# Hypergraph scatter in four rounded-type products, one attention tile later on TensorE

## The chip, the cores and the metric

The kernel runs on one core of a Trainium2 chip. The metric is the device time of one execution in microseconds; the kernel before takes 1202.09 us, the median of three runs (1201.91 to 1204.01).

## What is computed

The input is `x` of 16 batches x 512 nodes x 128 features and a 512x512 adjacency. Four graph layers follow each other, each with a layer norm, a ReLU and a residual. The edit is in the third, a hypergraph layer over 256 edges with given end nodes `src` and `dst` and 4 heads:

```python
# third layer (cut)
Xq = (H @ W_lin.T).reshape(bt, n, h, dh)
Xv = (H @ W_val.T).reshape(bt, n, h, dh)
e = jnp.einsum('behd,hd->beh', leaky_relu(Xq[:, src] + Xq[:, dst], 0.2), a)
e = e + jnp.log(A0[src, dst] + EPS)[None, :, None]
attn = softmax of e over the edges that share a src      # segment_max, exp, segment_sum
Y = segment_sum(attn[..., None] * Xv[:, dst], src, num_segments=n)   # the scatter
return Y @ W_out.T
```

The first layer is a graph ODE of 8 Euler steps, the second a masked graph attention, the fourth a Chebyshev propagation, a 4-head masked attention over all nodes and a feed-forward part. All work is in float32; where a product is made in the rounded type (float32r), the operand that is not exact in it is split into a rounded part and a rest.

## The kernel before

The program has two parts. The front (about 430 us) prepares tables and does the first layer for all batches, and already the first steps of batch 0. The rest treats the batches in a software pipeline of five stages: `gat`, `edge`, `cheb`, `att` and `ffn`, each one batch behind the one before. Each engine (TensorE is PE, VectorE DVE, ScalarE ACT, GpSimd POOL, and SP for the transfers) has a list of steps, written out by hand. `FILL_ORDER` (line 1685) is run once at the start, `ORDER` (line 1652) is the body of a loop with ten passes, and `DRAIN_ORDER` (line 1779) ends the program. An engine runs its list strictly in order, and a step waits on semaphores for what it needs. So the position of a step in a list decides what it holds up.

The steps around the edit, with their lines:

- `edge_u` (line 308, DVE) writes `U`, 128x256: the weighted values of the 256 edges, in two tiles of 128 edges.
- `edge_scatter` (line 370, PE) multiplies each tile of `U` by `src_rows`, a 0/1 table of 128 edges x 512 nodes, and adds both products in bank `b0`: two float32 products of 128x512. `src_rows` is filled by GpSimd in `edge_tables` (line 740). Earlier, the front keeps other data in the same memory (line 609).
- `edge_yT` (line 257, ACT) copies the result into `hg`, `edge_out` (line 377, PE) multiplies it by `W_out`, and `edge_x3` (line 315, DVE) adds the residual. `edge_x3` is the last DVE step of a pass. The next pass begins on DVE with `cheb_stats`, `cheb_aggr`, `gat_x2a`, `att_rv`.
- `att_turn` 0 to 15 (line 2442, PE) transpose the 16 attention tiles, all into one bank, `c2`. `att_copy` (line 2153, ACT) copies each out, so `att_turn` i waits for `att_copy` i-1. `att_score` (line 2434, PE), `att_mask` (line 2243, DVE) and `att_exp` (line 2145, ACT) make the tiles; each score feeds its mask, the mask its exponential.
- `att_rows` (line 2507, PE), early in the next pass, waits for `att_rv` (line 2318, DVE). `ffn_wo` (line 2529, PE) waits for `att_scale` (line 2322, DVE).
- On GpSimd a pass ends with `n3_rstd`, `ffn_x3b`, `n3_g` and `ffn_final` of the feed-forward stage.
- The edge gather (line 331, PE) already works in the rounded type: rounded part and rest of the nodes against a 0/1 table.

The PE order of a pass near its end is: `gat_pv0 att_turn11 att_score14 edge_scatter att_turn12 att_score15 edge_out att_turn13 gat_pv1 att_turn14 cheb_v`. On ACT it is `att_exp13 att_copy11 att_exp14 edge_yT att_copy12 att_exp15 att_copy13`.

Of the kernel before, what the change touches and what calls it, by code (L numbers as in the profile page):

```python
# [40 lines left out]
def need(eng, sem, value):  # L41
# [8 lines left out]
    edge_x edge_lcol edge_xz edge_le edge_exp edge_scattered edge_yT gat_done edge_stat edge_z edge_lb edge_max  # L50
    edge_lc edge_den edge_rden edge_attn edge_v edge_u x3_stored cheb_h edge_done ffn_y3 gat_turned gat_zloaded
    gat_loaded gat_aggr gat_vareps gat_rs gat_small gat_exp gat_s2 gat_hT gat_wh gat_pv gat_whs gat_max
    gat_eturn gat_eT gat_stat gat_normed gat_T gat_rinv
""".split()


# [5 lines left out]
def build(nc, t_in, out):  # L62
    ctx = ExitStack()
    with ctx:
        def sb(name, shape, dt=F32, c=None):
            return (c or ctx).enter_context(nc.sbuf_tensor(name, shape, dt))

        sems, kept = {}, {}

        def sem(name):  # L70

            if name not in sems:
                sems[name] = nc.alloc_semaphore(f"{name}_start")
# [24 lines left out]
        ones = sb("ones", [P, P])
        lap_hi = sb("lap_hi", [P, NT, N], R32)
        lap_lo = sb("lap_lo", [P, NT, N], R32)  # L100
        mask_gat = sb("mask_gat", [P, NT, N], BF16)
        mask_att = sb("mask_att", [P, NT, N], BF16)
        with ExitStack() as front:
            zsplit = sb("z_split", [P, 2, 2, N], R32, front)
        edge_pick = sb("edge_pick", [P, NT, 2 * E], R32)
        src_rows = sb("src_rows", [P, ET, N])
        seg_bias = sb("seg_bias", [P, ET, E])
        same_src = sb("same_src", [P, ET, E])
        logA = sb("logA", [P, ET])
        W = {n: sb("w_" + n, [P, D]) for n in ["Wc", "Wq", "Wk", "Wv", "Wo", "WlinT", "WvalT", "WoutT"]}  # L110
        W1 = sb("w_W1", [P, HID])
        W2 = sb("w_W2", [P, 2, D])
        rowv = sb("rowv", [P, len(ROWS), D])
        row = {n: rowv[:, i, :] for i, n in enumerate(ROWS)}
        b1c = sb("b1c", [P, 2])
        neg_half = sb("neg_half", [P, NT])
        W1ga = sb("w_W1ga", [P, D + 2])
        W["W1g"] = W1ga[:, 0:D]
        head_a4 = sb("head_a4", [P, H])

        def row4(name, c=NT):
            return row[name].unsqueeze(1).broadcast_to([P, c, D])

        k = Shared(t_in=t_in, out=out, bank=bank, sem=sem, kept_sem=kept_sem, nodes1=nodes1, row=row, row4=row4, W=W, W1=W1, W2=W2,
                   x1_dram=x1_dram, x3_dram=x3_dram, res_dram=res_dram, v_dram=v_dram, rowv=rowv, b1c=b1c,
                   ident=ident, ones=ones, neg_half=neg_half, lap_hi=lap_hi, lap_lo=lap_lo, mask_gat=mask_gat,
                   mask_att=mask_att, zsplit=zsplit, edge_pick=edge_pick, src_rows=src_rows, seg_bias=seg_bias,
                   same_src=same_src, logA=logA, W1ga=W1ga, head_a4=head_a4)

        k["gat"] = gat_memory(nc, ctx)
        k["edge"] = pair_memory(nc, k.gat)
        k["pair_words"] = 3 * NT * N + 4 * NT * D + 3 * E + ET * H * E // 2 + 6 * ET * H + ET * D + (6 + 2 + 4) * NT
        k["gat_steps"] = gat_stage(nc, k, kept_sem)
# [3 lines left out]
        nc.clear_and_free_semaphores(list(sems.values()))  # L140
# [44 lines left out]


def edge_stage(nc, k, sem):  # L190

    g = k.edge
    h2, x3, h2_hi, h2_lo, hg, xz, small, U = g.h2, g.x3, g.h2_hi, g.h2_lo, g.hg, g.xz, g.small, g.U
    zT, YT, x2, W = xz, hg, k.gat.x2, k.W
    b0, b1 = k.bank[4], k.bank[5]

    def cols(t):
        return slice(t * P, (t + 1) * P)
# [4 lines left out]
    def ready(eng, name, n, count=1, per=1):  # L203
        need(eng, sem(name), n * per + count)
# [10 lines left out]
    def on_gpsimd(pool):  # L215
# [13 lines left out]
            nc.gpsimd.tensor_tensor(h2_lo[:], h2[:], h2_hi[:].bitcast(F32), ALU.subtract  # L229
                                    ).then_inc(sem("edge_hlo"), 1)  # L230

        return {"edge_rstd": edge_rstd, "edge_lo": edge_lo}

    def on_scalar(act):
        def edge_apply(n):
# [88 lines left out]
    def on_tensor(pe):  # L324
# [43 lines left out]
            mm.then_inc(sem("edge_den"), 1)  # L368

        def edge_scatter(n):  # L370
            ready(pe, "edge_u", n)
            for e in range(ET):
                mm = nc.tensor.matmul(b0[:], U[:, cols(e)], k.src_rows[:, e, :], start=(e == 0),
                                      stop=(e == ET - 1))
            mm.then_inc(sem("edge_scattered"), 1)

        def edge_out(n):
# [189 lines left out]
def build_front(nc, k):  # L567
# [3 lines left out]
    with ExitStack() as c:  # L571
# [34 lines left out]
        S = [k.lap_hi, k.lap_lo]  # L606
        sqr = k.mask_att[:].rearrange("p t m -> p (t m)")

        gb = [k.src_rows[:].rearrange("p e n -> p (e n)")[:, i * D:(i + 1) * D] for i in range(STEPS)]
        gb.append(k.seg_bias[:, 0, 0:D])  # L610
        node_col = sb("node_col", [P, NT])
        edge_ci = sb("edge_ci", [P, 2, ET], I32)
# [108 lines left out]
        def _(pool):  # L721
# [934 lines left out]
        ffn_up0 att_score6 ffn_up1 att_turn4 att_score7 ffn_down0 ffn_down1 cheb_x1turn att_turn5 att_score8  # L1656
        edge_gather0 att_turn6 edge_gather1 att_score9 cheb_q edge_x att_turn7 att_score10 gat_eturn0 edge_lcol
        edge_lb0 edge_lb1 gat_eturn1 att_turn8 att_score11 cheb_k gat_eturn2 gat_eturn3 att_turn9 att_score12 edge_v
        edge_den att_turn10 att_score13 gat_pv0 att_turn11 att_score14 edge_scatter att_turn12 att_score15 edge_out
        att_turn13 gat_pv1 att_turn14 cheb_v  # L1660
    """.split(),
    "DVE": """
        cheb_stats cheb_aggr gat_x2a+ att_rv+ gat_x2b+ gat_stats att_mask0 gat_aggr edge_stats att_mask1 edge_aggr
# [8 lines left out]
        att_copy1 gat_wh_out1 edge_hi att_exp4 att_copy2 ffn_x2T att_exp5 att_copy3 ffn_gelu0 ffn_gelu1 att_exp6  # L1672
        att_copy4 att_exp7 att_copy5 cheb_x1T att_exp8 att_copy6 edge_hg gat_exp0 cheb_qsplit edge_xz att_exp9
        att_copy7 gat_exp1 gat_exp2 gat_exp3 gat_eT0 att_exp10 gat_eT1 att_copy8 att_exp11 edge_exp att_copy9 gat_eT2
        gat_eT3 cheb_ksplit att_exp12 att_copy10 att_exp13 att_copy11 att_exp14 edge_yT att_copy12 att_exp15
        att_copy13 att_copy14 att_copy15 cheb_vout att_spread
    """.split(),
    "POOL": """
        cheb_rstd gat_rstd edge_rstd ffn_res n2_rstd edge_lo ffn_b2 n1_rstd n3_rstd ffn_x3b n3_g ffn_final
    """.split(),  # L1680
    "SP": """
        load_z load_x3+ stack0+ stack2+ store_out+ load_xr stack1+ stack3+ edge_store+ load_x store_v+ cheb_res load_v
# [83 lines left out]
        cheb_rstd:0 gat_rstd:2 edge_rstd:1 n1_rstd:0 edge_lo:1 cheb_rstd:1 gat_rstd:3 edge_rstd:2 edge_lo:2 n1_rstd:1
        cheb_rstd:2 ffn_res:0 gat_rstd:4 edge_rstd:3 n2_rstd:0 ffn_b2:0 edge_lo:3 n1_rstd:2 n3_rstd:0 ffn_x3b:0 n3_g:0
        ffn_final:0 cheb_rstd:3 ffn_res:1 gat_rstd:5 edge_rstd:4 n2_rstd:1 ffn_b2:1 edge_lo:4 n1_rstd:3 n3_rstd:1
        ffn_x3b:1 n3_g:1 ffn_final:1
    """.split(),  # L1770
    "SP": """
        load_z:2 edge_store:0 cheb_res:0 load_x:2 load_z:3 stack0:0 stack2:0 edge_store:1 stack1:0 load_x:3 stack3:0
# [819 lines left out]
```

## Time and profile before

| | |
|---|---|
| median of 3 runs | 1202.09 us |
| profiled execution, first to last instruction | 1201.4 us |
| PE busy | 1124.4 us (94%) |
| DVE busy | 814.3 us (68%) |
| ACT busy | 759.7 us (63%) |
| POOL busy | 342.6 us (29%) |

The profile counts an instruction as busy from its start to its end. Products on PE overlap: the next one starts before the one before it has ended, so the distance of two starts tells what a product costs PE, and the duration when its result can be used. A float32 product of 128x512 shows as two records, one in the rounded type as one. The idle time that the profile gives before an instruction is put down to what ended it.

### The profile page before, as it was taken

To read this page: it belongs to the slowest core of one execution; us is meant where nothing else is said; L and a number is where in the kernel's file an instruction comes from. 1 tells how busy PE (TensorE), PEld (TensorE's weight loads), DVE (VectorE), ACT (ScalarE), POOL (GpSimd) and SP (SyncE) were. 2 spreads that over 40 slices of the span, in tenths; PEclk is the share of its full clock that TensorE was granted. 3 is DMA by queue.
4 is the path that set the end of the run, shared out by engine and by line. 5 is a ranking of instruction groups with operands and counts; after the bars stand their busy time and mean duration, and the time that the engine had idled before them with its cause. 6 is when DMAs were issued, how large, how long until landed. Compare 5 with 4: busy or idle time off the path is not lost. (4 is left out here: it accounts for less than half of the span.)

```text
span 1201.4 us, 23468 instructions
## 1 busy us (share of the span) xinstructions
PE 1124.4 (94%) x7537; PEld 898.6 (75%) x7537; DVE 814.3 (68%) x2964; ACT 759.7 (63%) x1627; POOL 342.6 (29%) x465
## 2 busy tenths in 40 slices
PE   8999999999999987999999999999999999999685
PEld 5678888889889865777777777777777777766454
DVE  7662222223335567798998988988988988977665
ACT  4324234334113234987988988988988988988762
POOL 3312005003032121133253243243243243243123
PEclk9999999999989998999999999999999999999987
DMA  4020120120110013243343343343343343233420
GB/s 130 24 56 1 45 62 1 45 62 1 56 33 9 28 36 92 71 111 96 90 116 90 88 118 89 88 115 92 88 114 94 88 114 94 81 106 86 122 67 27
DMA packets 132321, 87.85 MB, mean 73 GB/s; under 512 B 13600, under 2 KB 115360, under 8 KB 132256
## 3 DMA queue, kind: packets, MB, share of 16 engines
q1 hardware_dynamic: 132192, 87.02, 26.7%
q8 instruction: 36, 0.59, 0.2%
q14 instruction: 29, 0.24, 0.1%
q0 software_dynamic: 64, 0.00, 0.0%
HBM read 32.45 MB, written 20.97 MB: 44 GB/s over the span
## 5 line engine op out<-in xcount | busy, mean ns | idle before, releaser
L2247 DVE CUSTOM_DVE_ANT_0 att_Ts<-bank,mask_att 128x512 f32<-128x512 f32 x256 | 174.5, 683 | 63.6 <-PE bank L2402 61.2
L2149 ACT ACTIVATE att_Es<-att_Ts,att_small 128x512 f32<-128x512 f32 x256 | 185.4, 724 | 35.0 <-DVE att_small L2247 34.3
L2456 PE MATMUL bank<-ident,att_Es 128*128 128x128 f32 x1024 | 159.1, 279 | 16.8 <-ACT att_PTs L2158 12.3
L2158 ACT COPY att_PTs<-bank 128x512 f32<-128x512 f32 x248 | 144.0, 581 | 45.7 <-PE bank L2456 45.3
L2456 PEld LDWEIGHTS bank<-ident,att_Es 128*128 128x128 f32 x1024 | 121.7, 143 | 55.6 <-ACT att_PTs L2158 26.5
L2402 PE MATMUL bank<-K_parts,Q_parts 128*128 128x512 f32 x256 | 124.0, 494 | 3.7 <-DMA K_parts<-k_lo 2.3
L1943 POOL TENSOR_SCALAR n_rs<-n_mv 128x4 f32<-128x4 f32 x46 | 13.3, 289 | 306.4 <-DVE n_mv L1938 306.4
L985 DVE TENSOR_TENSOR P_row<-bank,l_bias 128x512 f32<-128x512 f32 x32 | 22.1, 691 | 86.1 <-PE bank L1440 68.0
L1430 PE MATMUL bank<-G,x0T 128*128 128x128 f32 x384 | 74.8, 276 | 0.7 <-DVE U2T L978 0.6
L1430 PE MATMUL bank<-G,U2T 128*128 128x128 f32 x384 | 74.2, 275 | 0.0
L1430 PE MATMUL bank<-G,U1T 128*128 128x128 f32 x384 | 74.2, 275 | 0.0
L729 POOL TENSOR_SCALAR l_rs<-l_mv 128x4 f32<-128x4 f32 x16 | 6.8, 425 | 214.5 <-DVE l_mv L969 214.2
L555 PE MATMUL bank<-gat_whs,gat_ETs 128*128 128x128 f32 x512 | 63.8, 280 | 2.0 <-PEq L141 2.0
L2402 PEld LDWEIGHTS bank<-K_parts,Q_parts 128*128 128x128 f32 x256 | 47.7, 191 | 23.1 <-issue 16.8
L1430 PEld LDWEIGHTS bank<-G,x0T 128*128 128x128 f32 x384 | 60.5, 191 | 4.2 <-issue 1.7
L555 PEld LDWEIGHTS bank<-gat_whs,gat_ETs 128*128 128x128 f32 x512 | 61.9, 196 | 2.3 <-issue 2.2
L1430 PEld LDWEIGHTS bank<-G,U2T 128*128 128x128 f32 x384 | 58.3, 192 | 0.0
L1430 PEld LDWEIGHTS bank<-G,U1T 128*128 128x128 f32 x384 | 58.3, 192 | 0.0
L978 DVE COPY U2T<-bank 128x512 f32<-128x512 f32 x16 | 11.0, 690 | 67.3 <-PE bank L1421 67.3
L2524 PE MATMUL bank<-att_PTs,v_in 128*32 128x512 f32 x480 | 55.4, 602 | 0.0
L440 ACT ACTIVATE gat_Ts<-gat_Vs,gat_small 128x512 f32<-128x512 f32 x64 | 45.7, 722 | 12.8 <-DVE gat_Vs L493 12.8
L1440 PE MATMUL bank<-Z_hi,P3T_hi 128*128 128x512 f32 x128 | 52.9, 414 | 0.0
(331 smaller groups left out, 2956.7 us busy)
## 6 DMA issues: line engine op xcount, KB each, us to landing
Q_parts<-q_hi SPq DMA_DIRECT2D x128, 64.0 KB, 2.0
Q_parts<-q_lo SPq DMA_DIRECT2D x128, 64.0 KB, 2.0
K_parts<-k_hi SPq DMA_DIRECT2D x128, 64.0 KB, 2.0
K_parts<-k_lo SPq DMA_DIRECT2D x128, 64.0 KB, 2.0
l_x<-in_x SPq DMA_DIRECT2D x16, 256.0 KB, 2.9
P2T<-in_x SPq DMA_DIRECT2D x16, 256.0 KB, 4.8
x_after_l<-P2T SPq DMA_DIRECT2D x16, 256.0 KB, 2.3
gat_z<-x_after_l SPq DMA_DIRECT2D x16, 256.0 KB, 3.3
```

The source lines that it names most:

```text
L440: nc.scalar.activation(g.T[:, t, :], g.V[:, t, :], ACT.Exp, scale=0.8, bias=small[:, 4, t:t + 1], accum_out=small[:, 6, t:t + 1]).then_inc ...
L555: mm = nc.tensor.matmul(a0[:, cols(t)], g.ET[:, s, cols(t)], WhA[:, s, 0:D], start=(s == 0), stop=(s == NT - 1))
L985: nc.vector.tensor_tensor(by_batch(zs[:, t, :]), by_batch(bank[t][:]), bias[:, BLOCKS - 1 - lev, t:t + 1, :].broadcast_to([P, CB, D]), ALU.add
L1430: mm = nc.tensor.matmul(bank[t][:, b * D:(b + 1) * D], UT[i][:, b, cols(t)], G[:, STEPS - k0 - i, :], start=(b == 0 and i == 0), stop=(lev ...
L1440: mm = nc.tensor.matmul(bank[t][:], left[:, s, cols(t)], right[:, s, :], start=False, stop=(s == NT - 1 and i == 2))
L1943: nc.gpsimd.tensor_scalar(rs[:, 0, :], mv[:, :, 1], EPS, None, ALU.add).then_inc(sem(tag + "_vareps"), 1)
L2149: nc.scalar.activation(att_E[:, j % RING_E, :], att_T[:, j % RING_T, :], ACT.Exp, scale=-1.0, bias=att_small[:, 0, j:j + 1], accum_out=att ...
L2158: nc.scalar.copy(att_PT[:, h, :, cols(q)], c2[:].rearrange("p (s q) -> p s q", q=P)).then_inc(sem("att_pt"), 1)
L2247: nc.vector.tensor_tensor_reduce(att_T[:, j % RING_T, :], [c0, c1][j % 2][:], k.mask_att[:, tile_of(n, j)[1], :], -QK_SCALE, HUGE, ALU.add ...
L2402: return nc.tensor.matmul(dst, left, right, start=True, stop=True)
L2456: mm = nc.tensor.transpose(dst[:, cols(s)], att_E[:, i % RING_E, cols(s)], k.ident[:])
L2524: mm = nc.tensor.matmul(b0[r, :], vD[:, s, r], att_PT[:, h, s, :], start=(s == 0), stop=(s == NT - 1))
```

## The change

- The scatter is done in the rounded type. `U` is split into `U_hi` (rounded) and `U_lo` (the rest), and each tile of `src_rows` is multiplied by both: four products of 128x512 instead of two in float32. `src_rows` becomes a rounded-type table; the other data in its memory get a name of their own, `fc_rows`, at the same place.
- The split is a new step `edge_parts` on GpSimd: a copy into `U_hi`, then a subtraction into `U_lo`, both 128x256. Both lie in the memory of `hg`, whose values are no longer needed then. It waits for `edge_u`; the scatter now waits for its end. On GpSimd it stands behind `n3_rstd` and ahead of `ffn_x3b` in the loop.
- In the loop's lists, the scatter goes behind `att_turn12 att_score15`, `edge_out` behind `gat_pv1`, and `edge_yT` on ACT behind `att_exp15`. In the lists of fill and drain, and in the front, the scatter keeps its place and `edge_parts` is added on GpSimd.

```diff
+        def edge_parts(n):
+            ready_alone(pool, "edge_u", n)
+            nc.gpsimd.tensor_copy(U_hi[:], U[:]).then_inc(sem("edge_uhi"), 1)
+            ready(pool, "edge_uhi", n)
+            nc.gpsimd.tensor_tensor(U_lo[:], U[:], U_hi[:].bitcast(F32), ALU.subtract).then_inc(sem("edge_ulo"), 1)
...
         def edge_scatter(n):
-            ready(pe, "edge_u", n)
+            ready(pe, "edge_ulo", n)
             for e in range(ET):
-                mm = nc.tensor.matmul(b0[:], U[:, cols(e)], k.src_rows[:, e, :], start=(e == 0),
-                                      stop=(e == ET - 1))
+                for i, part in enumerate([U_hi, U_lo]):
+                    mm = nc.tensor.matmul(b0[:], part[:, cols(e)], k.src_rows[:, e, :],
+                                          start=(e == 0 and i == 0), stop=(e == ET - 1 and i == 1))
             mm.then_inc(sem("edge_scattered"), 1)
...
     "PE": """
-        edge_den att_turn10 att_score13 gat_pv0 att_turn11 att_score14 edge_scatter att_turn12 att_score15 edge_out
-        att_turn13 gat_pv1 att_turn14 cheb_v
+        edge_den att_turn10 att_score13 gat_pv0 att_turn11 att_score14 att_turn12 att_score15 edge_scatter att_turn13
+        gat_pv1 edge_out att_turn14 cheb_v
...
     "ACT": """
-        gat_eT3 cheb_ksplit att_exp12 att_copy10 att_exp13 att_copy11 att_exp14 edge_yT att_copy12 att_exp15
+        gat_eT3 cheb_ksplit att_exp12 att_copy10 att_exp13 att_copy11 att_exp14 att_copy12 att_exp15 edge_yT
         att_copy13 att_copy14 att_copy15 cheb_vout att_spread
...
     "POOL": """
-        cheb_rstd gat_rstd edge_rstd ffn_res n2_rstd edge_lo ffn_b2 n1_rstd n3_rstd ffn_x3b n3_g ffn_final
+        cheb_rstd gat_rstd edge_rstd ffn_res n2_rstd edge_lo ffn_b2 n1_rstd n3_rstd edge_parts ffn_x3b n3_g ffn_final
```

## Rows read from the trace of the kernel before

**Rows 1.** Busy time by stretch, one pass of the loop (us, busy time and instructions):
```profile
core 0: us, PE busy (x) PEld busy (x) DVE busy (x) ACT busy (x) POOL busy (x), PEclk, DMA share, GB/s
690.23:735.46 45.23, 43.69 (x324) 34.01 (x323) 40.40 (x158) 39.52 (x89) 16.25 (x23) 1.00 0.36 99
```

**Rows 2.** Timeline of PE, end of a pass: start, us, engine, line, what, count:
```profile
734.72 0.60 PE L2456 MATMUL bank<-ident,att_Es 128*128 128x128 f32 x4
735.08 0.47 PE L2402 MATMUL bank<-K_parts,Q_parts 128*128 128x512 f32 x1
735.39 1.88 PE L373 MATMUL bank<-src_rows,edge_us 128*128 128x512 f32 x4
737.10 0.60 PE L2456 MATMUL bank<-ident,att_Es 128*128 128x128 f32 x4
737.46 0.47 PE L2402 MATMUL bank<-K_parts,Q_parts 128*128 128x512 f32 x1
737.95 1.16 PE L380 MATMUL bank<-w_WoutT,edge_hgs 128*128 128x128 f32 x8
738.95 0.60 PE L2456 MATMUL bank<-ident,att_Es 128*128 128x128 f32 x4
...
741.17 0.60 PE L2456 MATMUL bank<-ident,att_Es 128*128 128x128 f32 x4
...
743.50 1.08 PE L2402 MATMUL bank<-ident,att_small 128*32 128x128 f32 x32
```

**Rows 3.** Timeline of PE, first half of the edge gather (rounded type):
```profile
720.01 0.39 PE L331 MATMUL bank<-edge_pick,h_hi 128*128 128x512 f32 x1
720.24 0.40 PE L331 MATMUL bank<-edge_pick,h_lo 128*128 128x512 f32 x1
...
720.94 0.49 PE L2456 MATMUL bank<-ident,att_Es 128*128 128x128 f32 x3
```

**Rows 4.** Timeline of PE in the drain: two transposes with one score between:
```profile
1090.66 0.60 PE L2456 MATMUL bank<-ident,att_Es 128*128 128x128 f32 x4
...
1091.99 0.66 PE L2456 MATMUL bank<-ident,att_Es 128*128 128x128 f32 x4 [0.50 <-ACT att_PTs L2158]
```

**Rows 5.** Timeline of ACT, end of a pass:
```profile
735.36 0.59 ACT L2158 COPY att_PTs<-bank 128x512 f32<-128x512 f32 x1
736.47 0.72 ACT L2149 ACTIVATE att_Es<-att_Ts,att_small 128x512 f32<-128x512 f32 x1 [0.53 <-DVE att_small L2247]
...
737.30 0.60 ACT L259 ACTIVATE edge_hgs<-bank 128x512 f32<-128x512 f32 x1
737.80 0.58 ACT L2158 COPY att_PTs<-bank 128x512 f32<-128x512 f32 x1
```

**Rows 6.** Timeline of DVE, end of a pass and start of the next:
```profile
734.46 0.42 DVE L310 TENSOR_TENSOR edge_us<-bank,edge_small 128x256 f32<-128x256 f32 x1
...
738.12 0.69 DVE L2247 CUSTOM_DVE_ANT_0 att_Ts<-bank,mask_att 128x512 f32<-128x512 f32 x1 [1.68 <-PE bank L2402]
...
739.83 0.68 DVE L318 TENSOR_TENSOR x<-bank,x 128x512 f32<-128x512 f32 x1
...
742.39 0.24 DVE L2320 RECIPROCAL att_small<-att_small 128x16 f32<-128x16 f32 x1
...
748.08 0.69 DVE L2326 TENSOR_TENSOR att_oTs<-bank,att_row_scale 128x512 f32<-128x512 f32 x1
```

**Rows 7.** Instructions of POOL by line and form: busy us, mean ns, idle before:
```profile
L746 POOL TENSOR_SCALAR same_src<-edge_f,edge_c 128x256 f32<-128x256 f32 x2 | 1.9, 938 | 0.1
L2095 POOL TENSOR_TENSOR ffn_y2s<-ffn_y2s,rowv 128x256 f32<-128x256 f32 x2 | 1.4, 724 | 1.5 <-PE bank L2491 1.5
```

**Rows 8.** Timeline of PE, start of the next pass, `ffn_wo`:
```profile
749.39 1.05 PE L2398 MATMUL bank<-w_Wo,att_oTs 128*128 128x128 f32 x8
```

**Rows 9.** Timeline of DVE and PE, scatter of batch 2 in the fill:
```profile
506.65 0.42 DVE L310 TENSOR_TENSOR edge_us<-bank,edge_small 128x256 f32<-128x256 f32 x1
507.17 1.94 PE L373 MATMUL bank<-src_rows,edge_us 128*128 128x512 f32 x4
508.95 0.60 PE L2456 MATMUL bank<-ident,att_Es 128*128 128x128 f32 x4
```

More of the change, by code:

```diff
@@ L52 @@
     gat_loaded gat_aggr gat_vareps gat_rs gat_small gat_exp gat_s2 gat_hT gat_wh gat_pv gat_whs gat_max
-    gat_eturn gat_eT gat_stat gat_normed gat_T gat_rinv
+    edge_uhi edge_ulo gat_eturn gat_eT gat_stat gat_normed gat_T gat_rinv
 """.split()
@@ L105, in build @@
         edge_pick = sb("edge_pick", [P, NT, 2 * E], R32)
-        src_rows = sb("src_rows", [P, ET, N])
+        with ExitStack() as front:
+            fc_rows = sb("fc_rows", [P, ET * N], F32, front)
+        src_rows = sb("src_rows", [P, ET, N], R32)
         seg_bias = sb("seg_bias", [P, ET, E])
@@ L127, in build @@
                    mask_att=mask_att, zsplit=zsplit, edge_pick=edge_pick, src_rows=src_rows, seg_bias=seg_bias,
-                   same_src=same_src, logA=logA, W1ga=W1ga, head_a4=head_a4)
+                   same_src=same_src, logA=logA, fc_rows=fc_rows, W1ga=W1ga, head_a4=head_a4)
         k["gat"] = gat_memory(nc, ctx)
@@ L180, in sb @@
             return c.enter_context(nc.sbuf_tensor(name, shape, dt))
-        e = Shared(h2=sb("edge_hs", [P, NT, D]), x3=sb("x3", [P, NT, D]), h2_hi=sb("h2_hi", [P, NT, D], R32),
-                   h2_lo=sb("h2_lo", [P, NT, D], R32), hg=sb("edge_hgs", [P, 2 * E]), xz=sb("edge_xzs", [P, E]),
+        with ExitStack() as in_hg:
+            U_hi, U_lo = (in_hg.enter_context(nc.sbuf_tensor(n, [P, E], R32)) for n in ["edge_uhi", "edge_ulo"])
+        hg = sb("edge_hgs", [P, 2 * E])
+        e = Shared(U_hi=U_hi, U_lo=U_lo, hg=hg, h2=sb("edge_hs", [P, NT, D]), x3=sb("x3", [P, NT, D]), h2_hi=sb("h2_hi", [P, NT, D], R32),
+                   h2_lo=sb("h2_lo", [P, NT, D], R32), xz=sb("edge_xzs", [P, E]),
                    junk=sb("edge_junk", [P, ET * H, E], BF16), small=sb("edge_small", [P, 6, ET * H]),
@@ L194, in edge_stage @@
     zT, YT, x2, W = xz, hg, k.gat.x2, k.W
+    U_hi, U_lo = g.U_hi, g.U_lo
     b0, b1 = k.bank[4], k.bank[5]
@@ L230, in edge_lo @@
                                     ).then_inc(sem("edge_hlo"), 1)
-        return {"edge_rstd": edge_rstd, "edge_lo": edge_lo}
+        def edge_parts(n):
[3 more added lines that the diff above has]
+            nc.gpsimd.tensor_tensor(U_lo[:], U[:], U_hi[:].bitcast(F32), ALU.subtract).then_inc(sem("edge_ulo"), 1)
+        return {"edge_rstd": edge_rstd, "edge_lo": edge_lo, "edge_parts": edge_parts}
     def on_scalar(act):
@@ L607, in build_front @@
         sqr = k.mask_att[:].rearrange("p t m -> p (t m)")
-        gb = [k.src_rows[:].rearrange("p e n -> p (e n)")[:, i * D:(i + 1) * D] for i in range(STEPS)]
+        gb = [k.fc_rows[:, i * D:(i + 1) * D] for i in range(STEPS)]
         gb.append(k.seg_bias[:, 0, 0:D])
@@ L801, in _ @@
             gat["gat_rstd"](1)
+            edge["edge_parts"](0)
         @block.scalar
@@ L1622 @@
     "edge": """
+        edge_parts
         edge_lc
@@ L1765 @@
     "POOL": """
[L1766 to L1769, printed above, removed]
+        cheb_rstd:0 gat_rstd:2 edge_rstd:1 n1_rstd:0 edge_lo:1 edge_parts:1 cheb_rstd:1 gat_rstd:3 edge_rstd:2
+        edge_lo:2 n1_rstd:1 edge_parts:2 cheb_rstd:2 ffn_res:0 gat_rstd:4 edge_rstd:3 n2_rstd:0 ffn_b2:0 edge_lo:3
+        n1_rstd:2 n3_rstd:0 edge_parts:3 ffn_x3b:0 n3_g:0 ffn_final:0 cheb_rstd:3 ffn_res:1 gat_rstd:5 edge_rstd:4
+        n2_rstd:1 ffn_b2:1 edge_lo:4 n1_rstd:3 edge_parts:4 n3_rstd:1 ffn_x3b:1 n3_g:1 ffn_final:1
     """.split(),
@@ L1841 @@
     "POOL": """
-        cheb_rstd:14 ffn_res:12 edge_rstd:15 n2_rstd:12 edge_lo:15 ffn_b2:12 n1_rstd:14 n3_rstd:12 ffn_x3b:12 n3_g:12
-        ffn_final:12 cheb_rstd:15 ffn_res:13 n2_rstd:13 ffn_b2:13 n1_rstd:15 n3_rstd:13 ffn_x3b:13 n3_g:13
-        ffn_final:13 ffn_res:14 n2_rstd:14 ffn_b2:14 ffn_res:15 n2_rstd_0:15 n3_rstd:14 ffn_x3b:14 n3_g:14
+        cheb_rstd:14 ffn_res:12 edge_rstd:15 n2_rstd:12 edge_lo:15 ffn_b2:12 n1_rstd:14 n3_rstd:12 edge_parts:15
+        ffn_x3b:12 n3_g:12 ffn_final:12 cheb_rstd:15 ffn_res:13 n2_rstd:13 ffn_b2:13 n1_rstd:15 n3_rstd:13 ffn_x3b:13
+        n3_g:13 ffn_final:13 ffn_res:14 n2_rstd:14 ffn_b2:14 ffn_res:15 n2_rstd_0:15 n3_rstd:14 ffn_x3b:14 n3_g:14
         ffn_final:14 ffn_b2_0:15 n2_rstd_1:15 ffn_b2_1:15 n3_rstd_0:15 n3_rstd_1:15
```

## The prediction

> **What bounds the kernel now.** I read the engine table by stretch first. One pass of the loop over the batches takes 45.23 us, and in it TensorE (PE) is busy 43.69 us at a granted clock of 1.00, against 40.40 for VectorE (DVE), 39.52 for ScalarE (ACT) and 16.25 for GpSimd (POOL) [rows 1]. So PE is the bound, with little idle time, and work taken off it is worth something only where nothing else is already late behind it. Therefore I then read the timeline of PE at the place of the edit, and beside it those of ACT and DVE over the same microseconds. The reader is to see in rows 2 that each piece starts where the one before it has been issued: transpose `att_turn11` at 734.72, `att_score14` at 735.08, the scatter at 735.39, `att_turn12` at 737.10, `att_score15` at 737.46, `edge_out` at 737.95, `att_turn13` at 738.95 (and `gat_pv1` behind it), `att_turn14` at 741.17, and, after `cheb_v`, two scores and `att_turn15`, `att_rows` of the next pass at 743.50.
>
> **The cheaper passes.** The scatter takes 737.10 - 735.39 = 1.71 us of PE [rows 2]. The edge gather has the form of the new scatter: four rounded-type products of 128x512, at 720.01, ..., and the next work at 720.94, so 0.93 us for four [rows 3]. I take that: 0.78 us less PE work a batch, 16 x 0.78 = 12.5 us at most.
>
> **The split on GpSimd.** `edge_u` ends at 734.46 + 0.42 = 734.88 [rows 6]. The second instruction is a subtraction of 128x256, 0.72 us by the nearest row of that size on GpSimd [rows 7]. No row shows a plain copy there. It costs between nothing and the 0.94 us of the one-input 128x256 comparison [rows 7]; I take 0.72, the subtraction of equal size, which lies nearest in shape. With about 0.2 us for the two waits (an estimate) the rest is ready at 736.5, at the latest 736.75. The Trainium skill ("GPSIMD Engine Reference", section 4.1, Engine selection) speaks against this placement: two-input elementwise work belongs on VectorE, GpSimd being about twice as slow; here the same size takes 0.72 us on GpSimd against 0.42 for `edge_u` on VectorE, so the ratio is 1.7. The same table calls one-input work on GpSimd roughly line rate, which at the page's 1.2 GHz is an estimated 0.21 us for 256 elements; by that the copy would be 0.5 us shorter than I take and the sum below about 1 us smaller. Behind the new wait on GpSimd stand `ffn_x3b`, `n3_g` and `ffn_final`; they lie in time that GpSimd mostly idles, and the next pass's `cheb_rstd` is held by something later, below.
>
> **The move in the loop's PE list.** This is what decides. `att_turn12` writes the bank that `att_copy11` on ACT reads, so it waits for it. Before, the scatter covers that copy. Now only `att_score14` stands between. The drain already has this very order: transpose at 1090.66, score, next transpose at 1091.99, with idle time put down to the ACT copy [rows 4]. So `att_turn12` comes 1.33 us after `att_turn11`: 734.72 + 1.33 = 736.05. ACT is as ready here as there: the copy starts at 735.36, the moment `att_turn11` ends (734.72 + 0.60) [rows 2, 5]. PE loses 736.05 - 735.39 = 0.66 us. Then come `att_score15` (0.36 later, by 737.46 - 737.10) at 736.41 and the scatter at about 736.75, after 736.5, so GpSimd's wait is just covered. The scatter ends its issue at 737.68. `att_turn13` needs `att_copy12`, which stands on ACT behind `att_exp14`; that holds its place, since its score is not moved, and frees ACT at 737.30 [rows 5]. With 0.58 for the copy and 0.05 to PE: 737.93, another 0.25 us of idling. From there 2.22 us for `att_turn13` and `gat_pv1` (741.17 - 738.95) put `edge_out` at 740.15; `edge_yT` needs the scatter and `att_exp15`. The mask of that exponential, at 738.12 before, moves forward with its score by a microsecond to 737.1 [rows 6], so that `edge_yT`, behind the exponential, is done near 739.4 and not late. `edge_out` takes 0.86 us (an estimate: 1.00 from 737.95 to 738.95, less what its wait for `edge_yT` spread out), so `att_turn14` stands at 741.01 where it stood at 741.17. Of 0.78 us saved, 0.16 is left. The 2.33 us from `att_turn14` to `att_rows` (743.50 - 741.17) bring PE to `att_rows` at 743.34.
>
> **What is late next: `edge_x3` on DVE.** `edge_out` now ends at 740.15 + 0.86 + 0.16 = 741.17 (the tail: before, 737.95 + 1.16 = 739.11 against the next start 738.95). `edge_x3` follows at 741.21 instead of 739.83 [rows 6]: 1.38 us later. DVE runs its list in order: behind it are `cheb_stats`, `cheb_aggr`, `gat_x2a` and `att_rv`, which ended at 742.39 + 0.24 = 742.63, 2.80 us after `edge_x3` began, with no wait for another engine in between [rows 6]. Now 741.21 + 2.80 = 744.01, and `att_rows`, which waits for `att_rv`, starts at 744.06. PE stands still 0.72 us, and is 0.56 us later than before the change. DVE keeps its 1.38 us of lateness until `att_scale`, which ended at 748.08 + 0.69 = 748.77 and now ends at 750.15; `ffn_wo` was at 749.39 [rows 8], would be at 749.95 and waits until 750.20. So PE is 0.8 us late in all. Behind that the first wait of ACT for PE (`cheb_xT`) and of DVE for `ffn_wo` put all three at the same 0.8 us, and the next tail starts from the same relations. **One pass costs about 0.8 us more, 46.05 us.** Its bounds: without the two idle times in the tail everything behind them comes earlier by as much, 0.8 - 0.66 - 0.25 = -0.1; with a copy or a wait 0.1 to 0.2 worse than read, +1.0.
>
> **Beyond the loop.** The ten passes scatter batches 5 to 14. Nine are followed by such a start; in the last, the drain's list has `att_rv` right behind `edge_x3`, so nothing is late and 0.16 us is won. Batches 0 to 4 and 15 keep their place, so there the scatter waits for the split. For batch 2, `edge_u` ends at 506.65 + 0.42 = 507.07, the rest is ready 1.64 later at 508.71, and four passes end at 509.64, where the next transpose began at 508.95: +0.7 [rows 9]. The same sum gives, from the `edge_u` ends and the next starts of the other batches, +0.5, 0, +0.7, +0.3 and +0.7 for 0, 1, 3, 4 and 15. I count half of 0 and 15, the ends of the program, where less stands behind PE (an estimate): 2.3 us. With a free copy it is -0.6, with all of it and the dear copy 4.
>
> **The sum.** 9 x 0.8 - 0.2 + 2.3 = 9.3 us on the profiled execution's 1201.4 us span: 1210.7. Its median of three runs is 1202.09, 0.7 more than that span, so I say **1211 us**. The bounds: 9 x -0.1 - 0.6 = -1.5 and 9 x 1.0 + 4 = 13, so 1200.6 to 1215.
>
> **Rivals.** *PE's saving stays* (chance 0.13). If the lateness of `edge_out` were hidden, for instance because the next pass's `att_rows` were not held by `att_rv`, each batch would keep up to 0.78 us: 1202.1 - 12.5 = 1189.6 at best, and 1198.7 with the two idle times of the tail in ten passes (10 x 0.91 = 9.1). For it: PE is busy 43.69 of 45.23 us [rows 1]. Against it: `att_rows` had only 743.50 - 742.63 = 0.87 us to spare [rows 2, 6], and `edge_x3` moves by 1.38. *No difference* (0.15). The transposes wait less than the drain's rows say, because ACT and DVE settle differently, and the circle through `edge_x3` alone remains: about -0.1 us a pass, 1200.6 to 1203. *GpSimd sets the end* (0.07). The scatter is reached at 736.75 and the rest is ready at 736.5, so only a quarter of a microsecond is to spare. Two instructions that take over 2 us instead of 1.44 would delay the scatter; each further microsecond goes into every pass whole, past the 0.25 us that `att_turn13` waits anyway. At 0.7 us more that is 1211 + 10 x 0.45, some 1216. The forecast itself has 0.65.
>
> **How the numbers follow.** About 0.2% (2.4 us) is what a measurement of this kernel can tell from no change. Faster than that: 0.13; within: 0.15; slower: 0.72, the forecast and the GpSimd case together. The range takes in the bounds and the case of no difference and leaves out the fast case and the worst of the GpSimd one: 1200 to 1215.5.
>
> **What would show it.** In the profile after: the scatter as four records 0.23 us apart; `att_turn12` 1.33 us behind `att_turn11` with idle time put down to the ACT copy; `edge_x3` waiting for `edge_out` in every pass; PE idle before `att_rows`, put down to `att_rv`; passes of about 46 us with 43 us of PE work. I am wrong if passes are under 45.2 us, if `att_rv` ends before PE has come to `att_rows`, or if the scatter waits for GpSimd in the loop.

## The result and the profile after

| | before | after |
|---|---|---|
| median of 4 runs each, us | 1203.05 (1201.91 to 1204.85) | 1211.60 (1209.28 to 1215.57) |
| profiled execution, first to last instruction, us | 1201.4 | 1207.5 |
| one pass of the loop, us | 45.23 | 46.28 |
| PE busy in a pass, us | 43.69 | 43.31 |

The ratio of the times is 1.0079 (95%: 1.0059 to 1.0099). The kernel became slower: by 8.6 us between the medians, by about 9.5 us by the ratio. 1211 was forecast, 1211.60 was measured.

**The pass.** Busy time by stretch of the kernel after, for the pass that answers to [rows 1]:

```profile
core 0: us, PE busy (x) PEld busy (x) DVE busy (x) ACT busy (x) POOL busy (x), PEclk, DMA share, GB/s
689.25:735.53 46.28, 43.31 (x324) 33.88 (x323) 40.21 (x158) 39.53 (x89) 17.97 (x25) 1.00 0.36 96
```

PE has less work and the pass is 1.05 us longer, so PE stands still for longer. Where it does is in its timeline, end of a pass, the kernel after; it answers to [rows 2]:

```profile
733.52 0.60 PE L2471 MATMUL bank<-ident,att_Es 128*128 128x128 f32 x4
733.88 0.47 PE L2417 MATMUL bank<-K_parts,Q_parts 128*128 128x512 f32 x1
734.80 0.66 PE L2471 MATMUL bank<-ident,att_Es 128*128 128x128 f32 x4 [0.45 <-ACT att_PTs L2173]
735.21 0.47 PE L2417 MATMUL bank<-K_parts,Q_parts 128*128 128x512 f32 x1
735.53 0.40 PE L386 MATMUL bank<-src_rows,edge_uhi 128*128 128x512 f32 x1
735.76 0.39 PE L386 MATMUL bank<-src_rows,edge_ulo 128*128 128x512 f32 x1
...
736.62 0.65 PE L2471 MATMUL bank<-ident,att_Es 128*128 128x128 f32 x4
737.11 1.95 PE L568 MATMUL bank<-gat_whs,gat_ETs 128*128 128x128 f32 x16
738.90 1.06 PE L393 MATMUL bank<-w_WoutT,edge_hgs 128*128 128x128 f32 x8
739.79 0.60 PE L2471 MATMUL bank<-ident,att_Es 128*128 128x128 f32 x4
...
742.95 1.08 PE L2417 MATMUL bank<-ident,att_small 128*32 128x128 f32 x32 [0.76 <-DVE att_small L2335]
```

`att_turn12` stands 1.28 us behind `att_turn11` (734.80 - 733.52), with idle time put down to the ACT copy. The scatter's products are 0.23 us apart and wait for nobody. `att_turn14` comes 6.27 us after `att_turn11` (739.79 - 733.52), where it came after 6.45 [rows 2]: of the 0.78 us that PE saved 0.18 is left. Then `att_rows` waits 0.76 us for the reciprocal of `att_rv`. VectorE over the same stretch, beside [rows 6]:

```profile
739.99 0.69 DVE L330 TENSOR_TENSOR x<-bank,x 128x512 f32<-128x512 f32 x1 [2.32 <-PE bank L393]
740.72 0.87 DVE L1946 BATCH_NORM_STATS2 cheb_stat<-x 128x6 f32<-128x128 f32 x4
741.74 0.38 DVE L1953 BATCH_NORM_AGGREGATE cheb_mv<-cheb_stat 128x2 f32<-128x6 f32 x4
742.04 0.61 DVE L521 SCALAR_TENSOR_TENSOR x<-bank,gat_small,gat_xin 128x128 f32<-128x128 f32 x2
742.57 0.24 DVE L2335 RECIPROCAL att_small<-att_small 128x16 f32<-128x16 f32 x1
```

`edge_x3` starts 6.47 us after `att_turn11` (5.11 before), and the reciprocal ends 2.82 us later (742.81 - 739.99), with no wait for another engine in between: this is the circle that the prediction went by. The split itself is on GpSimd:

```profile
733.86 0.40 POOL L240 CAST edge_uhi<-edge_us 128x256 fp32r<-128x256 f32 x1 [0.57 <-DVE edge_us L322]
734.34 0.73 POOL L242 TENSOR_TENSOR edge_ulo<-edge_us,edge_uhi 128x256 fp32r<-128x256 f32 x1
```

It is done at 735.07, 0.46 us ahead of the scatter at 735.53. It waited for this step of DVE, which ended at 733.69:

```profile
733.27 0.42 DVE L322 TENSOR_TENSOR edge_us<-bank,edge_small 128x256 f32<-128x256 f32 x1
```

**What else PE waits for in a pass.** The feed-forward's `ffn_down` waits for its GELU on ACT. PE, then ACT, in the kernel after:

```profile
761.79 2.05 PE L2562 MATMUL bank<-w_W,ffn_mT 128*128 128x128 f32 x16 [1.23 <-ACT ffn_mT L2157]
```
```profile
757.01 0.60 ACT L2149 ACTIVATE ffn_mT<-bank 128x512 f32<-128x512 f32 x1
757.87 0.72 ACT L2164 ACTIVATE att_Es<-att_Ts,att_small 128x512 f32<-128x512 f32 x1 [0.26 <-DVE att_small L2262]
...
759.17 1.28 ACT L2157 ACT_TABLE_LOAD   x1
760.47 1.27 ACT L2157 ACTIVATE ffn_mT<-bank,b1c 128x512 f32<-128x512 f32 x2
```

and the same PE step before:

```profile
761.92 2.05 PE L2547 MATMUL bank<-w_W,ffn_mT 128*128 128x128 f32 x16 [0.98 <-ACT ffn_mT L2142]
```

The wait grew from 0.98 to 1.23 us, because an exponential ahead of the GELU on ACT now waits 0.26 us for its mask on DVE. DVE is late because `ffn_y2` waits for GpSimd. DVE, then POOL, in the kernel after:

```profile
750.75 0.69 DVE L2346 TENSOR_TENSOR ffn_y2s<-bank,ffn_xr 128x512 f32<-128x512 f32 x1 [0.70 <-POOL ffn_xr L2098]
```
```profile
747.49 1.63 POOL L228 TENSOR_TENSOR edge_rs<-edge_rs,neg_half 128x4 f32<-128x4 f32 x1
...
749.35 1.29 POOL L2098 TENSOR_TENSOR ffn_xr<-ffn_xr,rowv 128x512 f32<-128x512 f32 x1
```

and POOL, then DVE, before:

```profile
747.31 1.04 POOL L222 TENSOR_TENSOR edge_rs<-edge_rs,neg_half 128x4 f32<-128x4 f32 x1
...
748.58 1.28 POOL L2083 TENSOR_TENSOR ffn_xr<-ffn_xr,rowv 128x512 f32<-128x512 f32 x1
```
```profile
750.48 0.69 DVE L2331 TENSOR_TENSOR ffn_y2s<-bank,ffn_xr 128x512 f32<-128x512 f32 x1
```

Counted from `att_rows` (742.95 after, 743.50 before), `ffn_res` (the last row) starts at 6.40 instead of 5.08. Of these 1.32 us, 0.59 are the longer power (1.63 against 1.04), and the other 0.73 are DVE's lateness, by which its statistics come later. Which kernels have the longer power is in the last section.

**The account of a pass.** From `att_turn11` to `att_rows` it takes 9.43 us (742.95 - 733.52) instead of 8.78: +0.65. `cheb_prop`, behind `ffn_wo`, starts at 749.79, 6.84 after `att_rows` (750.20 - 743.50 = 6.70 before): +0.14, as `ffn_wo` waits for `att_scale`. The two starts of `cheb_prop` on PE, in the kernel after and in the one before:

```profile
749.79 0.48 PE L2424 MATMUL bank<-lap_hi,h_hi 128*128 128x512 f32 x1
```
```profile
750.20 0.48 PE L2409 MATMUL bank<-lap_hi,h_hi 128*128 128x512 f32 x1
```

The GELU brings +0.25 (1.23 - 0.98). Together 1.04, of the 1.05 us by which the passes differ.

**The account of the whole.** Read from the starts of `edge_x3`, which close each batch's hypergraph layer. Where the scatter stands in fill and drain it waits for the split, as in this row of PE (batch 3, the kernel after):

```profile
548.87 0.50 PE L386 MATMUL bank<-src_rows,edge_uhi 128*128 128x512 f32 x1 [1.43 <-POOL edge_ulo L242]
```

| | before | after | difference |
|---|---|---|---|
| start to batch 0 | 431.33 | 426.69 | -4.64 |
| batch 0 to 4 | 172.60 | 173.94 | +1.34 |
| batch 4 to 5 (first pass) | 45.43 | 46.82 | +1.39 |
| batch 5 to 14 (nine passes) | 407.10 | 416.54 | +9.44 |
| batch 14 to 15 (drain) | 43.26 | 42.14 | -1.12 |
| batch 15 to the end | 101.7 | 101.4 | -0.3 |

Summed, +6.1: the difference of the two spans. The first row is not the change's. In the eleven profiled executions of this case, one for each kernel, the first `edge_x3` lies anywhere from 425.3 to 433.9 us, and its place goes with TensorE's mean granted clock over the first 50 us: 425.3 to 426.7 in the four with 1.00 (the kernel after is one), 430.2 to 431.3 in the three with 0.97 (the kernel before is one), 432.8 to 433.9 in the four with 0.93. Kernels that differ from the one after in the loop's lists alone are in all three groups. A single span therefore can't tell a few microseconds; the length of a pass, which agrees to 0.04 us within an execution, can. From batch 0 on the change costs 10.7 us.

The ratio carries this too: 55 executions of the kernel before, timed beside the experiments, took 1195.9 to 1201.0 us at a mean granted clock of 0.980 or more and 1201.7 to 1206.0 at 0.978 or less, and those of the kernel after 1209.3 to 1213.0 at 0.981 (three) and 1215.6 at 0.977 (one), so that at like clock the change costs some 11 us (the medians of each group against each other), nearer to the 10.7 than the ratio is.

The rows +1.39 and -1.12 are mostly one thing: within a pass `edge_x3` stands 1.36 us later, so the distance grows where the loop is entered and shrinks where it is left. In the row of batch 0 to 4, 0.91 of the 1.34 us lie between batch 2 and 4 (92.34 against 91.43), and six more kernels with the same fill have 92.34 to 92.39 there. The rest lies between batch 0 and 2, where these seven kernels differ by 1.5 us (81.60 to 83.09) and a few tenths can't be told.

### The profile page after: what moved, and what is told of

Same layout as the page of the kernel before. It is cut to its first block and busy times, and to the rows that moved or that the text cites. A ratio compares the mean times of both kernels' runs of the same rounds, so it can differ in the third digit from the quotient of the medians.

```text
span 1207.5 us, 23510 instructions
## 1 busy us (share of the span) xinstructions
PE 1110.2 (92%) x7537; PEld 892.4 (74%) x7537; DVE 815.0 (67%) x2964; ACT 759.8 (63%) x1627; POOL 365.1 (30%) x497
```

## Experiments

Two things were asked: which part of the change costs the time, and whether the circle over `edge_out`, `edge_x3` and `att_rv` decides, as predicted. The first rival is that the split on GpSimd sets the pace, the second that the wait of `att_turn12` alone is to blame. All edits are to the kernel after unless said otherwise; the pass is read at a steady place of the loop.

| run | pass, us | time, ratio to before (95%) |
|---|---|---|
| before | 45.23 | |
| after | 46.28 | 1.0079 (1.0059 to 1.0099) |
| e1_split_old_lists | 45.45 | 1.0064 (1.0037 to 1.0092) |
| e2_move_alone | 46.85 | 1.0116 (1.0063 to 1.0169) |
| e3_out_before_pv1 | 45.33 | 1.0046 (1.0019 to 1.0073) |
| e4_rv_first | 46.20 | 1.0125 (1.0054 to 1.0195) |
| e5_pv_quarters | 45.18 | 1.0036 (1.0014 to 1.0058) |
| e6_split_dearer | 46.55 | one execution, 1227.85 us |
| e7_res_earlier | 46.97 | one execution, 1216.32 us |
| e8_out_early_quarters | 45.10 | 1.0042 (1.0016 to 1.0068) |
| e9_fill_drain_too | 45.10 | 1.0013 (0.9994 to 1.0032) |

A time is longer than its pass alone tells, since the fill with the split stays in it: from batch 0 to batch 5 it takes 218.03 us before, 221.14 in e1_split_old_lists and 220.73 in e3_out_before_pv1.

**The split without the move.**

```diff
-  PE: att_turn11 att_score14 att_turn12 att_score15 edge_scatter att_turn13 gat_pv1 edge_out att_turn14
+  PE: att_turn11 att_score14 edge_scatter att_turn12 att_score15 edge_out att_turn13 gat_pv1 att_turn14
-  ACT: att_exp14 att_copy12 att_exp15 edge_yT
+  ACT: att_exp14 edge_yT att_copy12 att_exp15
```

> The four rounded passes and the split on GpSimd stay, the loop's lists on PE and ACT are those of before (scatter ahead of att_turn12, edge_yT ahead of att_copy12, edge_out ahead of att_turn13). Theory, that the move costs the time and not the split: in the changed kernel the rest of U was ready 1.38 us after edge_u ended; in the frame of before that is 736.26, so the scatter waits 0.9 us for GpSimd, runs from 736.3 to 737.35, and att_turn12 stands 0.25 us later than before; a pass takes 45.5 us, with no idle time before att_rows put down to att_rv; fill and drain cost 2 us as in the changed kernel; about 1207.5 us in all. Rival, that the split on GpSimd costs the time (its wait, or the work it delays there): a pass as in the changed kernel, 46.3 us, about 1211 us.

The pass took 45.45 us. PE in this kernel:

```profile
737.64 0.48 PE L2417 MATMUL bank<-K_parts,Q_parts 128*128 128x512 f32 x1
738.87 0.50 PE L386 MATMUL bank<-src_rows,edge_uhi 128*128 128x512 f32 x1 [0.75 <-POOL edge_ulo L242]
...
739.90 0.60 PE L2471 MATMUL bank<-ident,att_Es 128*128 128x128 f32 x4
```

From `att_score14` to `att_turn12` it takes 2.26 us (739.90 - 737.64), 2.02 before [rows 2]: the wait for GpSimd takes all that the cheaper products save and 0.24 more, and the pass is longer by just that (0.22). So in the old place the split can't win, and the move, made to it, adds the other 0.83 of the 1.05.

**The move without the split** (the kernel before with the new order of PE and ACT, `U` still as float32).

> The kernel before with the new loop lists of PE and ACT alone: the scatter stays in float32 (two products, 1.71 us) and waits for edge_u. Theory: the move alone costs more than the whole change, since the scatter is 0.78 us longer and 0.16 us of that are hidden by the wait for att_copy12: a pass of 46.28 + 0.6 = 46.9 us, idle time before att_turn12 of about 0.45 and before att_rows of about 0.8 us; nothing lost in fill and drain; about 1218 us. Rival, that the split on GpSimd costs the time: a pass of 45.2 to 45.3 us, about 1203 us.

46.85 us, 1.62 more than before. The new order is the expensive part; in it the cheaper products give back 0.57 of their 0.78. PE in this kernel shows the same two waits as after:

```profile
734.47 0.66 PE L2456 MATMUL bank<-ident,att_Es 128*128 128x128 f32 x4 [0.44 <-ACT att_PTs L2158]
735.20 1.88 PE L373 MATMUL bank<-src_rows,edge_us 128*128 128x512 f32 x4
...
743.18 1.08 PE L2402 MATMUL bank<-ident,att_small 128*32 128x128 f32 x32 [0.75 <-DVE att_small L2320]
```

**`edge_out` back ahead of `gat_pv1`.** This leaves the wait of `att_turn12` and takes away only the lateness of `edge_x3`. Two places change together: `edge_out` on PE and, with it, the copy `edge_yT` that it needs on ACT.

```diff
-  PE: edge_scatter att_turn13 gat_pv1 edge_out att_turn14
+  PE: edge_scatter att_turn13 edge_out gat_pv1 att_turn14
-  ACT: att_copy12 att_exp15 edge_yT
+  ACT: att_copy12 edge_yT att_exp15
```

> The changed kernel with edge_out ahead of gat_pv1 on PE and edge_yT ahead of att_exp15 on ACT. Theory, that the loss is edge_x3 being late behind edge_out: edge_out ends 1.6 us earlier (about 0.2 us of waiting for edge_yT), edge_x3 stands at its old place, the 0.76 us before att_rows and the 0.41 us behind it (ffn_wo, ffn_down) go, the idle time before att_turn12 stays: a pass of 45.3 us, about 1205.5 us in all. Rival, that the loss is the wait of att_turn12 for the copy of the tile before: a pass stays at 46 us or more, about 1210 us.

45.33 us. PE in this kernel:

```profile
740.52 0.66 PE L2471 MATMUL bank<-ident,att_Es 128*128 128x128 f32 x4 [0.44 <-ACT att_PTs L2173]
...
743.02 1.16 PE L393 MATMUL bank<-w_WoutT,edge_hgs 128*128 128x128 f32 x8
744.02 1.95 PE L568 MATMUL bank<-gat_whs,gat_ETs 128*128 128x128 f32 x16
...
748.13 1.08 PE L2417 MATMUL bank<-ident,att_small 128*32 128x128 f32 x32
```

`att_turn12` still waits 0.44, `att_rows` no longer at all, and 0.95 of the 1.05 us is gone. This tells the theory from the second rival: the place of `edge_out`, with its copy, decides.

**`att_rv` first on DVE.** If only `att_rows` were held, its reciprocal right behind `edge_x3` would free it.

```diff
-  DVE: cheb_stats cheb_aggr gat_x2a+ att_rv+ gat_x2b+
+  DVE: att_rv+ cheb_stats cheb_aggr gat_x2a+ gat_x2b+
```

> The changed kernel with att_rv first in the next pass's DVE list, right behind edge_x3. Theory, that all of DVE's list is late and not only att_rv: the idle time before att_rows (0.76 us) goes, but att_scale ends where it did, so ffn_wo waits for it some 0.7 us instead of 0.04; a pass of 46.2 us, about 1211 us. Rival, that only the place of att_rv behind three other steps costs the time: a pass of 45.5 us, about 1205 us.

46.20 us, only 0.08 less. PE in this kernel:

```profile
749.45 1.08 PE L2417 MATMUL bank<-ident,att_small 128*32 128x128 f32 x32
...
754.92 0.66 PE L534 MATMUL bank<-ident,gat_z 128*128 128x128 f32 x4 [0.53 <-DVE gat_z L481]
```

`att_rows` doesn't wait, and the next step that needs DVE, `gat_turn`, waits 0.53 instead (some 0.7 was expected, at `ffn_wo`). The whole list behind `edge_x3` is late, not one step of it.

**A dearer split.** The subtraction is done twice in each batch.

> The changed kernel with the subtraction on GpSimd done twice, some 0.8 us more ahead of the scatter. Theory: in the changed kernel the rest was ready 0.4 us before PE reached the scatter, and 0.16 us more is lost afterwards anyway while att_turn13 waits for its copy; so of 0.8 us about 0.3 reach a pass: 46.6 us. Rival, that GpSimd already sets the place of the scatter: the 0.8 us go into a pass whole, 47.1 us. If GpSimd had time to spare throughout: 46.3 us.

46.55 us, 0.27 more than after. PE in this kernel:

```profile
749.79 0.50 PE L388 MATMUL bank<-src_rows,edge_uhi 128*128 128x512 f32 x1 [0.23 <-POOL edge_ulo L244]
```

About 0.8 us of GpSimd work was added, and 0.27 of it arrives. GpSimd had some 0.5 us to spare; the rival that it sets the pace in the loop falls. In the fill it is otherwise: there the scatters of batches 1 to 4 each wait 0.8 us longer for the split, as here for batch 2 (1.07 in the kernel after),

```profile
512.20 0.78 PE L388 MATMUL bank<-src_rows,edge_uhi 128*128 128x512 f32 x1 [1.87 <-POOL edge_ulo L244]
```

and from batch 0 to batch 5 it takes 227.15 us instead of 220.76.

**`ffn_res` earlier.** A test of the GELU's part.

```diff
-  POOL: cheb_rstd gat_rstd edge_rstd ffn_res
+  POOL: cheb_rstd gat_rstd ffn_res edge_rstd
```

> The changed kernel with ffn_res ahead of edge_rstd in GpSimd's loop list. In the changed kernel ffn_y2 on DVE waits 0.70 us for ffn_res, and the wait of ffn_down for the gelu grew by 0.26 us. Theory, that the first causes the second: ffn_y2 waits no more, ffn_down starts 0.26 us earlier in the pass, a pass of 46.0 us. Rival, that the feed-forward steps are late by DVE's own list: a pass stays at 46.3 us.

46.97 us, where 46.0 was expected: a miss. `ffn_y2` doesn't wait any more and the GELU's wait is back at 0.97 us, as expected. But now these two stand beside each other on DVE and POOL, in this kernel:

```profile
747.37 2.08 DVE L481 TENSOR_SCALAR gat_z<-gat_z,gat_mv,gat_rs 128x128 f32<-128x128 f32 x4
```
```profile
747.30 1.29 POOL L2098 TENSOR_TENSOR ffn_xr<-ffn_xr,rowv 128x512 f32<-128x512 f32 x1
```

`gat_apply` takes 2.08 us; in the kernel after, where `ffn_res` does not run beside it, 1.12:

```profile
746.50 1.12 DVE L481 TENSOR_SCALAR gat_z<-gat_z,gat_mv,gat_rs 128x128 f32<-128x128 f32 x4
```

It was not expected, and it puts PE to a wait at `gat_turn`, here in the kernel of this run:

```profile
749.50 0.66 PE L534 MATMUL bank<-ident,gat_z 128*128 128x128 f32 x4 [0.74 <-DVE gat_z L481]
```

So the gain of 0.26 is confirmed in its place and buried by another delay.

**Towards a better version.** `gat_pv` is cut into four parts of about 0.9 us, which lie between the transposes so that the ACT copies are covered (the lists are shown, the code of the new steps is not).

```diff
-  PE: att_score13 gat_pv0 att_turn11 att_score14 att_turn12 att_score15 edge_scatter att_turn13 gat_pv1 edge_out
+  PE: att_score13 gat_pvq0 att_turn11 att_score14 gat_pvq1 att_turn12 att_score15 edge_scatter att_turn13
+      gat_pvq2 edge_out gat_pvq3
-  ACT: att_copy12 att_exp15 edge_yT
+  ACT: att_copy12 edge_yT att_exp15
```

> The changed kernel with gat_pv cut into its four node tiles, put one each behind att_score13, att_score14, att_turn13 and edge_out, and edge_yT ahead of att_exp15. Theory: with 0.9 us of other work between att_turn11 and att_turn12 the wait for the copy goes (a part of it returns before att_turn11, whose copy stands behind two other steps on ACT), edge_out stands near its old place, edge_x3 0.1 us later than before, and the saving of the rounded passes shows: a pass of 44.7 to 44.9 us (before 45.23), about 1200 us with the 2 us of fill and drain. Rival, that another engine has become the bound: 45.2 us or more.

45.18 us, 0.3 to 0.5 worse than expected. `att_turn12` is covered, but `att_turn11`, with half the cover that it had, waits 0.45 us for its copy, and the GELU's wait is at 1.25, as in the kernel after (1.23 to 1.25). Next, scatter and `edge_out` go a step earlier still:

```diff
-  PE: gat_pvq1 att_turn12 att_score15 edge_scatter att_turn13 gat_pvq2 edge_out gat_pvq3
+  PE: gat_pvq1 att_turn12 edge_scatter att_score15 att_turn13 edge_out gat_pvq2 gat_pvq3
```

> The kernel with gat_pv in quarters, and in it the scatter ahead of att_score15 and edge_out right behind att_turn13, ahead of the last two quarters. Quarters alone left a pass at 45.18 us, with 0.34 us given back where ffn_down waits for the gelu, because edge_x3 was still about half a microsecond later in the pass than before. Theory, that what counts is where edge_out ends: edge_x3 comes 0.7 us earlier than with quarters alone, ffn_y2 waits less for GpSimd, the 0.34 us go, and 0.1 us is lost at edge_out for edge_yT: a pass of 45.0 us; about 1202 us with the fill and drain of the changed kernel. Rival, that PE or the copies of the tiles bound the tail whatever the order: 45.2 us.

45.10 us, the GELU's wait at 0.98. That is 0.13 us a pass better than before the change, although `att_turn11` still waits 0.45. No run has the quarters with the float32 scatter, so it isn't shown that the gain comes from the cheaper products. In time this kernel is still slower, and a part of that lies in the fill: 220.64 us from batch 0 to batch 5, 218.03 before. In fill and drain the scatters of batches 2, 3 and 15 were therefore set behind other PE work:

```diff
-  PE: gat_eturn3:3 edge_scatter:2 att_turn12:0
+  PE: gat_eturn3:3 att_turn12:0 edge_scatter:2
-  PE: edge_scatter:3 att_turn11:1 cheb_v:2 att_score14:1 edge_out:3 att_turn12:1 att_score15:1
+  PE: att_turn11:1 cheb_v:2 edge_scatter:3 att_score14:1 att_turn12:1 edge_out:3 att_score15:1
-  PE: att_turn13:13 edge_scatter:15 att_turn14:13 edge_out:15 att_score0:14 att_score1:14
+  PE: att_turn13:13 att_turn14:13 edge_scatter:15 att_score0:14 att_score1:14 edge_out:15
-  ACT: edge_yT:3 att_copy11:1
+  ACT: att_copy11:1 edge_yT:3
```

> As the kernel before this one, and in the fill and drain lists the scatter of batches 2, 3 and 15 goes behind another piece of PE work (a transpose, a transpose and cheb_v, a transpose), edge_out of 3 and 15 and one copy with it. Theory: the scatter waits there for GpSimd 1.1 to 1.4 us each in the changed kernel, and of it some 0.7 us a batch reach the end; with other work in the wait about 2 us of fill and drain go: the distance between edge_x3 of batch 0 and of batch 5 shrinks by 1 to 1.5 us, the pass stays at 45.0 us, about 1200 us and 0.2% under the kernel before. Rival, that these waits lie beside other idle time: nothing changes.

The scatters of batches 2 and 3 no longer wait, but the gain is missed. From batch 0 to 5 it takes 220.02 us, 0.6 less than in the run above, where 1 to 1.5 less was expected, and 2.0 more than before. The 0.6 lie between batch 0 and 2, the stretch that can't tell tenths; from batch 2 to 5 it is 137.69 us, 137.72 in the run above. PE in this kernel shows why:

```profile
510.60 0.66 PE L2478 MATMUL bank<-ident,att_Es 128*128 128x128 f32 x4 [0.70 <-ACT att_PTs L2180]
...
555.51 0.66 PE L2478 MATMUL bank<-ident,att_Es 128*128 128x128 f32 x4 [1.19 <-ACT att_PTs L2180]
```

In the scatters' place two transposes now wait for their ACT copies, which the scatter had covered, and `edge_out` of batch 3 starts 43.55 us behind the `edge_x3` of batch 2 (558.68 - 515.13), where it was 42.30 before (554.80 - 512.50). The move costs here what it costs in the loop: from batch 2 to 3 it takes 46.74 us, 45.92 before. The other 1.2 us over before lie between batch 0 and 2 (82.33 against 81.17), with a spread of 1.5 us there. For batch 15 there is no gain either: 43.93 us from batch 14 to 15, 43.64 in the run above. In time, this kernel can't be told from the one before.

## Why the prediction was right

- *PE's saving:* four products 0.23 us apart, 0.92 us in all; 0.93 was taken.
- *The wait of `att_turn12`:* 1.28 us behind `att_turn11`, 1.33 taken from the drain [rows 4]. `att_turn13`'s second idle time was taken as 0.25; here it starts 0.17 us past the scatter's end (736.62 against 736.22 + 0.23).
- *What is left at `att_turn14`:* 0.18 us; 0.16 forecast. *`edge_x3`:* 1.36 us late; 1.38 forecast. *`att_rows`:* waits 0.76 us and stands 0.65 late; 0.72 and 0.56 forecast. The runs with `edge_out` put back and with the move alone show that this circle is the cause, and not only beside it.
- *`ffn_wo`:* 0.25 forecast, 0.14 measured.
- *A term that was missing:* 0.25 us for the GELU. The text said that GpSimd's late start in the next pass is held by something later, and stopped there; `ffn_res`, at the end of that row, had 0.62 us to spare before (it ended at 748.58 + 1.28 = 749.86, and `ffn_y2` started at 750.48) and came 1.32 late, 0.59 of it by a longer power that the text did not have either. The forecast of 0.81 a pass so met 1.05.
- *The split:* the copy took 0.40 us and not 0.72, the two with their waits 1.38 (735.07 - 733.69) instead of 1.64; the two waits are 0.25 of that (0.17 and 0.08), taken as 0.2. The Trainium skill ("GPSIMD Engine Reference", section 4.1, Engine selection) calls one-input work there roughly line rate, 0.21 by the estimate in the prediction; the measured 0.40 lies above that and well below the 0.72 taken. In the loop it changed nothing, as the split was covered either way. The prediction's remark that a copy of 0.21 would make its sum about 1 us smaller does not follow from its own list of batches: 0.5 us less for each gives nearly 2.
- *Fill and drain:* 2.1 forecast, with the last pass; 1.3 measured behind batch 0. For batch 2 the scatter waits 1.07 us in the kernel after, and the step behind it starts 2.71 us behind the step ahead of it (504.75 - 502.04) instead of 2.21 (508.95 - 506.74): 0.5 later, with 0.7 forecast. For batch 3, where it waits 1.43, it is 2.94 (549.91 - 546.97) instead of 2.04 (553.24 - 551.20): 0.9, with 0.7 forecast, though the copy is cheaper; there GpSimd was still at the power of `n3_rstd` when `edge_u` was done. Together 1.4; from batch 0 to 4 the table has 1.34.
- *The sum:* nine passes gave 9.44 where 7.2 was forecast, the ends 1.3 where 2.1 was. The forecast of 9.3 us met 10.7 behind batch 0 and about 9.5 in the ratio of the times. Part of that closeness is luck: the two errors have opposite signs, and at like clock the change costs some 11 us.
- *Rivals:* the saving did not stay. GpSimd does not set the end in the loop, though the scatter waits for it where the old order was kept: in the fill, and in e1_split_old_lists. "No difference" rested on transposes that wait less than in the drain; they wait as long.

## What to carry to other kernels

A cheaper step on the bounding engine is worth what the order around it lets through: price the move that makes room for it before the saving itself, by following the moved step's result through the other engines' lists until it comes back. In a loop, one step that ends a pass late makes the whole list behind it late, and pulling a single consumer ahead only hands the wait to the next one. Read each engine's slack to its end, the helper engine's too: "held by something later" is a reason to go on reading.

## What the runs showed of the hardware

- **VectorE is slower beside GpSimd.** Four SBUF-to-SBUF scalings of 128x128 on DVE took 2.08 us beside a GpSimd addition of 128x512, and 1.12 where it did not run beside them. The longest single scaling of this line was 1.31 us in e7_res_earlier, about as long as the addition, and 0.35 in the kernel after. The addition itself took 1.29 us in both. The Trainium skill ("Advanced Engine Details and Errata", VectorE Performance Modes, Mode Summary) says that VectorE's second SBUF port is shared with GpSimd, so that GpSimd's instructions and VectorE's in a two-port mode block each other. That VectorE takes longer agrees; that these scalings use the second port, and that it is the cause, was not tested by itself.
- **A power of 128x4 on GpSimd** took 1.63 us in the kernel after and 1.04 before, with the same shape. Which it is goes with the start of DVE's `cheb_lo`, a subtraction from SBUF to SBUF, here in the kernel after and in the one before:

```profile
747.53 0.69 DVE L2227 TENSOR_TENSOR h_lo<-cheb_hs,h_hi 128x512 fp32r<-128x512 f32 x1
```
```profile
747.46 0.69 DVE L2212 TENSOR_TENSOR h_lo<-cheb_hs,h_hi 128x512 fp32r<-128x512 f32 x1
```

It starts 0.04 us behind the power after (747.53 - 747.49) and 0.15 before (747.46 - 747.31). In the loops of five kernels (after, e2_move_alone, e4_rv_first, e5_pv_quarters, e6_split_dearer) it starts 0.04 to 0.06 us behind the power, and the power takes 1.63; in five (before, e1_split_old_lists, e3_out_before_pv1, e8_out_early_quarters, e9_fill_drain_too) 0.12 to 0.39 behind, and it takes 1.04. Kernels with the split and without it are in both groups, so the split is not the reason. In e7_res_earlier it is 1.76 at 0.19, behind the slowed `gat_apply`. No run moved `cheb_lo` by itself, so why a tenth of a microsecond counts stays open.
